# Layer 0's expert blocks in eight turns of nine, with scatters ahead of them, fetches and adding up behind them, and the capacity search at three bits a turn

## The reference, cut to what is computed

```python
xn = _layernorm(x, axis=-1)
x = x + _L0_attn_ref(xn, ...) + _L0_ffn_ref(xn, ...)   # 16 rows of 256 tokens; t = 4096
...
def _L0_ffn_ref(x, Wr, W1, W2):                        # EMBED 128, FFN 512, N_EXPERTS 8, TOP_K 2
    probs = jax.nn.softmax(xf @ Wr, axis=-1)
    topk_probs, topk_experts = jax.lax.top_k(probs, TOP_K)
    cap = max(math.ceil(t * TOP_K * CAP_FACTOR / N_EXPERTS), 1)      # 1280
    for e in range(N_EXPERTS):
        ...
        vals, idx = jax.lax.top_k(g_masked, cap)
        g = jnp.where(jnp.isfinite(vals), vals, 0.0)
        h = jax.nn.relu(xf[idx] @ W1[e]) @ W2[e]
        y = y.at[idx].add(g[:, None] * h)
```

## Time and profile before

| what | value |
|---|---|
| median of 3 runs | 2079.53 us (2074.1 to 2083.88) |
| the profiled execution | 2077.18 us, span 2074.8 us |
| PE busy | 1624.0 us, 78% of the span |
| DVE, ACT, POOL busy | 1238.6, 766.0, 380.3 us |
| mean granted TensorE clock | 0.86 |
| stretches | layer 0 to about 662 us, layer 1 to about 1070, layer 2 to about 1610, then layer 3 |

### The profile page before, as it was taken

The page is one execution under the profiler, slowest core; times in us unless marked ns, Lnnn a source line. Parts: engine busy times, 40 slices in busy tenths (PEclk is TensorE's granted clock), DMA queues, the critical chain, the costliest instruction groups (busy, mean ns, idle before and its releaser), DMA issues.

```text
span 2074.8 us, 44343 instructions
## 1 busy us (share of the span) xinstructions
PE 1624.0 (78%) x12567; PEld 1050.6 (51%) x12567; DVE 1238.6 (60%) x3512; ACT 766.0 (37%) x1723; POOL 380.3 (18%) x488
## 2 busy tenths in 40 slices
PE   3257999999972599998983588888887688888888
PEld 3123666666632577877872244444543344444444
DVE  6454666566675665665574455555557566666664
ACT  2013445445441222322230254445454144434444
POOL 1274101101167011111123300000006200000000
PEclk9855999999965698988885598999997599999999
DMA  7023455455421000000001332333232111111110
GB/s 233 28 70 101 141 155 174 137 157 174 130 58 37 0 1 1 0 0 0 0 1 40 89 95 89 98 112 110 82 95 57 36 39 42 40 40 39 37 40 15
DMA packets 133278, 144.90 MB, mean 70 GB/s; under 512 B 15001, under 2 KB 114130, under 8 KB 132946
## 3 DMA queue, kind: packets, MB, share of 16 engines
q1 hardware_dynamic: 127058, 131.37, 21.4%
q0 software_dynamic: 6144, 12.60, 2.1%
HBM read 104.65 MB, written 39.52 MB: 69 GB/s over the span
## 4 chain that ended last, share of the span: by engine, by line
PE 48%; DVE 19%; issue 13%; DMA 8%; POOL 7%; SPq 2%; ACT 2%; DVEq 1%; ACTq 0%; POOLq 0%
PE pO L694 6%; DMA stk<-packed_qk 6%; PE pT_ L557 5%; PE pH L584 5%; PE pY L592 5%; DVE X L1278 4%; PE pH L500 4%; POOL sorted_x L910 3%; PE pS L642 3%; PE pS L664 3%; DVE mx L1239 2%; PE pT_ L490 2%; PE pY L512 2%; PE pT_ L555 2%; DVE stk L1245 2%
## 5 line engine op out<-in xcount | busy, mean ns | idle before, releaser
L804 ACT ACTIVATE pex<-pT_ 128x512 f32<-128x512 f32 (+1 forms) x768 | 426.6, 562 | 656.1 <-PE pT_ L557 362.8
L1239 DVE TENSOR_REDUCE mx<-pS 128x2 f32<-128x512 f32 x512 | 348.2, 688 | 194.9 <-PE pS L540 176.8
L557 PE MATMUL pT_<-stk 32*128 32x256 f16 x1024 | 208.2, 298 | 120.0 <-DMA stk<-packed_qk 67.0
L540 PE MATMUL pS<-stk 32*128 32x256 f16 x1024 | 220.3, 304 | 23.4 <-DMA stk<-packed_qk 19.6
L694 PE MATMUL pO<-pex,va 128*9 128x256 f32 (+1 forms) x3072 | 218.4, 408 | 2.0 <-ACT pex L804 2.0
L797 ACT ACTIVATE wb<-pH,b 128x256 f32<-128x256 f32 x256 | 107.3, 470 | 268.4 <-PE pH L500 268.4
L883 POOL TENSOR_TENSOR qk<-qkf,qk 128x512 f16<-128x512 f32 x48 | 55.4, 1155 | 779.5 <-DVE qk L1211 407.3
L557 PEld LDWEIGHTS pT_<-stk 32*128 32x128 f16 x1024 | 55.9, 94 | 238.0 <-issue 87.3
L500 PE MATMUL pH<-XT,w 128*128 (+1 forms) x512 | 146.7, 413 | 0.0
L584 PE MATMUL pH<-xsT,wb 128*128 128x128 f32 x888 | 134.1, 297 | 0.0
L1245 DVE SCALAR_TENSOR_TENSOR stk<-pS,stk 128x512 f16<-128x512 f32 x96 | 66.3, 691 | 109.2 <-PE pS L664 105.0
(11 more groups left out here) (195 smaller groups left out, 2841.5 us busy)
## 6 DMA issues: line engine op xcount, KB each, us to landing
wb<-in_w SPq DMA_DIRECT2D x111, 514.0 KB, 3.8
stk<-packed_qk SPq DMA_DIRECT2D x96, 256.0 KB, 2.8
packed_qk<-qk SPq DMA_DIRECT2D x144, 128.0 KB, 2.0
xsb<-sorted_x SPq DMA_DIRECT2D x111, 64.0 KB, 3.4
sorted_y<-ysb SPq DMA_DIRECT2D x111, 64.0 KB, 3.1
sorted_x<-wb SPq DMA_DIRECT2D x2, 2048.0 KB, 13.3
w<-in_w SPq DMA_DIRECT2D x2, 1024.0 KB
out<-X SPq DMA_DIRECT2D x16, 128.0 KB, 1.8
```

The lines of the kernel that those rows point to most:

```text
L540: return pe.matmul(bank[:, part * T:(part + 1) * T], stk[rows, side, j, part * P:(part + 1) * P], stk[rows, side, j, T:2 * T], start=True, ...
L557: return pe.matmul(bank[:, part * T:(part + 1) * T], key, stk[rows, side, j, 0:T], start=True, stop=True)
L804: act.activation(pex[:, k % 8, 0:n], bank[:, 0:n], ACT.Exp).then_inc(s("T_free"), 1)
L1239: ins = dve.tensor_reduce(mx[:, :, j, col], bank.rearrange("p (c n) -> p c n", c=2), AX.X, ALU.max)
```

## The change

Layer 0's 72 blocks come in turns 3 to 10, nine each, and the ring of loads has 3 places. Scatters: 6 behind turn -2, 13 in turn -1 (at S), 15 each in turns 0, 1 and 2 (at D). Fetches: one a head in turns 11 to 15. DVE adds 28 of the 32 tiles in turns 12 to 15, one every second head, and 4 behind the turns. The search does three bits a turn in turns 1 to 10 (a C and four c steps each) and the choice among equal ones is in turn 11. Layer 0's loop runs over turns 3 to 10, the others' as before. The places are zeroed 24 blocks at a time, since wb is smaller. Layer 2 keeps its plan.

```diff
-IN_FLIGHT = {0: 4, 2: 3}
+IN_FLIGHT = {0: 3, 2: 3}
...
-BLOCKS_A_TURN = {0: 6, 2: 3}
-BLOCK_TURNS = {0: range(2, 14), 2: range(1, 14)}
-SORT_TURNS = {0: range(-2, 2), 2: range(-2, 0)}
-SEARCH_STEPS = 6
-CAPACITY_TURN = 14
-
-GATHERS_A_HEAD = {14: 3, 15: 4}
-TILES_A_HEAD = {0: 1, 2: 2}
+ZEROED_BLOCKS = 24
+BLOCKS_A_TURN = {0: 9, 2: 3}
+BLOCK_TURNS = {0: range(3, 11), 2: range(1, 14)}
+SCATTERS = {0: {-2: 6, -1: 13, 0: 15, 1: 15, 2: 15}, 2: {-2: 16, -1: 16}}
+SEARCH_STEPS, SEARCHES_A_TURN = 5, 3
+SEARCH_TURNS = range(1, 11)
+CAPACITY_TURN = 11
+
+GATHER_FROM = {0: (11, 0), 2: (14, 2)}
+GATHERS_A_HEAD = {0: {11: 1, 12: 1, 13: 1, 14: 1, 15: 1}, 2: {14: 3, 15: 4}}
+COMBINE_FROM = {0: 12, 2: 15}
...
-LOOP_FROM, LOOP_TO = 2, 14
+LOOPS = {0: (3, 11), 1: (2, 14), 2: (2, 14), 3: (2, 14)}
...
-            if layer == 0 and n in SEARCH_TURNS and h % 8 < SEARCH_STEPS:
+            if layer == 0 and n in SEARCH_TURNS and h < SEARCHES_A_TURN * SEARCH_STEPS:
...
-                k, part = divmod(h, 8)
+                k, part = divmod(h, SEARCH_STEPS)
...
-                    sorting = l in SORTED and turn.loop is None and turn.n in SORT_TURNS[l]
+                    sorts = SCATTERS[l].get(turn.n, 0) if l in SORTED and turn.loop is None else 0
+                    gathers_now = GATHERS_A_HEAD[l].get(turn.n, 0) if l in SORTED and turn.loop is None else 0
+                    if gathers_now:
+                        pool.wait_ge(s("S_free"), PRIMED + turn.use("S"))
+                        pool.wait_ge(s("row_staged"), PRIMED + min(B, turn.n + 2))
                     for kind, k, local in turn.steps:
-                        if sorting and turn.n > -2 and kind == "S":
+                        if kind == ("S" if turn.n < 0 else "D") and k < sorts and turn.n > -2:
                             scatter(1)
...
                         if kind == "D":
-                            if l in SORTED and turn.loop is None and turn.n in GATHERS_A_HEAD and (turn.n, k) >= (14, 2):
-                                gather(GATHERS_A_HEAD[turn.n])
+                            if gathers_now and (turn.n, k) >= GATHER_FROM[l]:
+                                gather(gathers_now)
...
-                    if sorting and turn.n == -2:
-                        scatter(NT // 2)
+                    if turn.n == -2:
+                        scatter(sorts)
...
-                for part in {1: (1, 2), 2: (3,), 3: (4,), 4: (5,), 5: (6,)}[k]:
+                for part in {1: (1, 2), 2: (3,), 3: (4,), 4: (5, 6)}[k]:
...
+            def combined_at(l, n, h):
+                turns = B - COMBINE_FROM[l]
+                first, last = ((NT * (H * (n - COMBINE_FROM[l]) + hh)) // (H * turns) for hh in (h, h + 1))
+                return [t for t in range(first, last) if t < 2 * (B - 2)]
...
-            for c in range(0, MAXBLOCKS, NT):
-                n = min(NT, MAXBLOCKS - c)
+            for c in range(0, MAXBLOCKS, ZEROED_BLOCKS):
+                n = min(ZEROED_BLOCKS, MAXBLOCKS - c)
```

More of the change, by code:

```diff
@@ L63 @@
 MAXBLOCKS = max(BLOCKS.values())
-BLOCKS_A_TURN = {0: 6, 2: 3}
-BLOCK_TURNS = {0: range(2, 14), 2: range(1, 14)}
-SORT_TURNS = {0: range(-2, 2), 2: range(-2, 0)}
-SEARCH_STEPS = 6
-CAPACITY_TURN = 14
-GATHERS_A_HEAD = {14: 3, 15: 4}
-TILES_A_HEAD = {0: 1, 2: 2}
+ZEROED_BLOCKS = 24
[8 more added lines that the diff above has]
+COMBINE_FROM = {0: 12, 2: 15}
 GATHERS = 8
 WROW = 2 * FF + NF
-SEARCH_TURNS = range(-1, 14)
 def blocks_of(layer, n):
@@ L207, in use, with run_turns @@
         return self.loop * (2 * ring_uses(self.layer, ring, self.n)) + before
-def run_turns(eng, layer, body, loop_to=LOOP_TO):
+def run_turns(eng, layer, body, unlooped=0):
     last = B if layer == 1 else B + 1
-    for n in range(-2, LOOP_FROM):
+    loop_from, loop_to = LOOPS[layer][0], LOOPS[layer][1] - unlooped
+    for n in range(-2, loop_from):
         body(Turn(layer, n))
-    with eng.Fori(0, (loop_to - LOOP_FROM) // 2) as loop:
+    with eng.Fori(0, (loop_to - loop_from) // 2) as loop:
         for par in range(2):
-            body(Turn(layer, LOOP_FROM + par, loop))
+            body(Turn(layer, loop_from + par, loop))
     for n in range(loop_to, last):
@@ L245, with __init__ @@
 class TurnChain(Chain):
-    def __init__(self, eng, sem):
+    def __init__(self, eng, sem, layer):
         super().__init__(eng, sem)
         self.total, self.counts = 0, {}
+        self.loop_from, self.loop_to = LOOPS[layer]
     def enter(self, turn):
@@ L256, in enter @@
         else:
-            per = self.counts[LOOP_FROM - 1]
+            per = self.counts[self.loop_from - 1]
             self.base = turn.loop * (2 * per) + self.total
@@ L264, in leave @@
         if self.turn.loop is not None:
-            assert self.n == self.counts[LOOP_FROM - 1], (self.n, self.counts)
-            if self.turn.n == LOOP_FROM + 1:
-                self.total += self.n * (LOOP_TO - LOOP_FROM) - self.n
+            assert self.n == self.counts[self.loop_from - 1], (self.n, self.counts)
+            if self.turn.n == self.loop_from + 1:
+                self.total += self.n * (self.loop_to - self.loop_from) - self.n
                 return
@@ L598, in take_turn @@
                     elif kind == "C":
-                        pe.wait_ge(sem("counted"), PRIMED + turn.count(2, k + 3))
+                        first = SEARCHES_A_TURN * SEARCH_TURNS[0] - 1
+                        pe.wait_ge(sem("counted"), PRIMED + turn.count(SEARCHES_A_TURN, k - first))
                         pe.matmul(bank[:, 0:8], onesm[:, :], cnt[:, :], start=True, stop=True)\
@@ L845, in _ @@
                     pool.wait_ge(sem("gates"), PRIMED + l + 1)
-                split = TurnChain(pool, sem(f"L{l}_pool_chain"))
+                split = TurnChain(pool, sem(f"L{l}_pool_chain"), l)
                 def stage(turn, par):
@@ L922, in gather @@
                             pool.wait_ge(sem(f"ys_out{ring}"), PRIMED + 16 * n_out)
-                        pool.wait_ge(s("S_free"), PRIMED + Turn(l, 14).use("S"))
-                        pool.wait_ge(s("row_staged"), PRIMED + B)
                     for t, choice in gathers[:n]:
@@ L936, in _ @@
                     if l == 0:
-                        pool.wait_ge(sem("places_zeroed"), 16 * -(-MAXBLOCKS // NT))
+                        pool.wait_ge(sem("places_zeroed"), 16 * -(-MAXBLOCKS // ZEROED_BLOCKS))
                     pool.wait_ge(sem("places_ready"), 1 + SORTED.index(l))
@@ L1229, in take_turn @@
                     elif kind == "D":
-                        if l in SORTED and turn.n == B - 1:
-                            n_add = TILES_A_HEAD[l]
-                            combine(l, final, stats, [t for t in range(n_add * k, n_add * (k + 1)) if t < 2 * (B - 2)])
+                        if l in SORTED and turn.n >= COMBINE_FROM[l]:
+                            combine(l, final, stats, combined_at(l, turn.n, k))
                     elif kind == "S":
@@ L1366, in _ @@
                 final, stats = {}, {}
-                tc = TurnChain(dve, sem(f"L{l}_dve_chain"))
+                tc = TurnChain(dve, sem(f"L{l}_dve_chain"), l)
                 run_turns(dve, l, lambda turn: take_turn(turn, tc))
@@ L1370, in _ @@
                 if l in SORTED:
-                    combine(l, final, stats, range(min(TILES_A_HEAD[l] * H, 2 * (B - 2)), NT + 2))
+                    combine(l, final, stats, range(2 * (B - 2), NT + 2))
         primed = [n for n in sems if n in SHARED_SIGNALS or (n.startswith("L") and not n.endswith("_chain"))]
@@ L1461, in _ @@
                     sp.wait_ge(sem("fixed_rows"), 16 * (1 + l // 3))
-                run_turns(sp, l, sp_turn, LOOP_TO - 2)
+                run_turns(sp, l, sp_turn, 2)
             sp.wait_ge(sem("stored"), 16 * B)
```

## The result

The changed kernel takes 2411.45 us (median of 4 runs, 2405.8 to 2414.66) against 2078.12 us of the kernel before: 1.160 times as long, 95% interval 1.1563 to 1.1635. The prediction said slower, 2369 us, range 2265 to 2455. The direction and the mechanism came out as forecast; one term of the sum, the clock, was too small by a third.

A forecast was written before the change was run, and what follows sets the result against it. PE bounds the turns with blocks (busy 29.0 of 30.7 us). Layer 0's turns sum to 821.6 against 486.9 us, +334.7; with -12.2 and -30.5 that is +292.0 on 2077.2: 2369 us, range 2265 to 2455.

The forecast's parts named there:

- the clock: Turns 3 to 10: four waits of 3.8 us or more lower PE's clock, 2.6 us each, 10.2 a turn.
- The ring of three: Turns with nine blocks: X waits for tokens whose load only an earlier Y lets go, 25.1 us a turn.
- Rival 2's first half: Turns with nine blocks: all seven waits of over 1 us lower the clock, 18.2 a turn, 2433 us; chance 0.15.
- Rival 1: Turns with nine blocks: waits cost only themselves, no clock is lost, 63.4 us a turn, 2287 us; chance 0.15.
- rival 2's second half: Turns with nine blocks: work between waits can't win the clock back, 90.5 us a turn, 2504 us; chance 0.10.
- Rival 3: Turns with nine blocks: the load is covered ahead of X6 and X7, 38.3 us a turn, 2087 us; chance 0.05.
- Rival 4: Layer 0's ends: blockless turns take longer (+25) or the tail stays (+30), 2390 to 2420 us; chance 0.10.
- The head: Turn 0 starts 12.2 us earlier, with 6 scatters on POOL after turn -2 instead of 16.
- The first turn with blocks: PE's 9.6 us wait for the last scatter and the low clock around it stay, 12 us added.
- Turns 1 and 2, 14 and 15: Layer 0's blockless turns: turns 1 and 2 take 29.6 us each, turns 14 and 15 take 40.4 together.
- The end: Behind layer 0's attention: all fetches are out by turn 14, next layer begins at 631.5 instead of 662.0, -30.5 us.

The follow-up runs named there:

- Experiments 1: Changed kernel with tokens of block k+3 issued behind X of block k, only the weights behind Y: 2114.02 us, 1.0189 of the kernel before.
- 2: Kernel before with a ring of three alone, places zeroed 24 blocks at a time: 2355.98 us, 1.1351 of the kernel before.
- 11: Kernel before with a ring of three and tokens of block k+3 let go by X of block k instead of Y: 2073.85 us, 0.9987.
- experiment 3: Changed kernel with the two DMAs of a load swapped, tokens ahead of weights: 2260.78 us, 1.0896 of the kernel before.
- experiment 12: Kernel before with 6 scatters instead of 16 behind turn -2, the ten left over in turn 1: 2076.71 us, 0.9987.

## Why the prediction was right, and where it was short

Profiled against profiled, the steps of the sum:

```
                                   predicted   measured
turn 0 starts earlier by                12.2       12.6
turn 0                                  26.4       26.3
turns 1 and 2                           59.2       63.9
eight turns with nine blocks           600.8      629.3
  of it first one longer by               12        5.3
  a turn: PE's work                     38.3       38.3 (taken from the forecast)
  a turn: waits for tokens              25.1       25.4
  a turn: the clock                     10.2       15.0
turn 11                                 35.6       36.3
turns 12 and 13                         59.2       60.0
turns 14 and 15                         40.4       46.8
first to last exponential              821.6      862.6
gain at the end                         30.5       29.9
```

*The ring of three* held as worked out. The prediction put waits at X3 to X8 and X1, none at X0 and little at X2; the trace has seven a turn, 25.4 us against 25.1. One by one, in turn 5, X3 to X8 wait 3.5, 3.3, 1.8, 4.7, 4.6 and 4.3 us and X1 2.3, where the forecast had 2.8, 3.8, 2.4, 4.7, 4.7, 4.4 and 1.7. Experiments 1, 2 and 11 show it from three sides: take the rule away and 297 us go, put the ring alone into the kernel before and 279 come, and put both in and nothing is lost.

*The clock* is the step that was mis-sized: 15.0 us a turn (78.7 - 38.3 - 25.4; 15.5 by PE's busy time, see experiment 1) where I had 10.2. The price of one wait was near, and the number of them wrong. I let only the four waits of 3.8 us or more lower the clock, at 2.6 each, since layer 2's 3.1 us were the shortest that I had seen do it. The windows of six us behind each wait show which of them pay: 55 of the 57 in the changed kernel (all but one of 1.3 and one of 1.8 us), all 44 in experiment 2, of which the shortest was 1.7 us, and 34 of the 49 in experiment 3. Spread over these, the cost is 2.2, 2.4 and 2.4 us each, near the 2.6 of the forecast. No wait of over 2.2 us went without a stretch at 0.50 behind it; of the shorter ones some did, and no run here shows what decides it. Rival 2's first half said nearly that, all seven waits at 2.6, for 2433 us; the measurement is 22 below it and 42 above my number. The Trainium skill (TensorE: Matmul & The Clock Gate, HAM oscillation — how this bites in real kernels) tells of a kernel whose waits for a DMA, about 3 to 5 us each, let every tile restart at the half rate; the long waits here agree with it, and the shorter ones, down to 1.4 us in the changed kernel, lie outside what it tells and mostly pay as well. Rival 1 (no clock cost, 2287) falls with the mean of 0.70. So does rival 2's second half (half clock throughout, 2504): by that mean 60% of the time was at half.

*Rival 3*, the load covered, was rightly held for unlikely, and experiment 1 is that case made: 2114 us where I had 2087. 18 of the difference lie in layer 0 (its block turns 1.4 us longer each, and 9 us in the turns without blocks), the rest behind it.

*Rival 4*, that the ends don't pay (2390 to 2420), has the measured 2411 in its band, but not for its reason: the turns without blocks took 12.5 us more than forecast, not 25, and the gain at the end came.

*The head.* Turn 0 starts 12.6 us earlier, so the step was right; experiment 12 shows that in the kernel before it would have been worth nothing, because the last scatter sets when blocks start. The sum could subtract the 12.2, since it adds the third turn ahead of the blocks (32.8 us) elsewhere, but a gain it is not in the change either: the last scatter is issued at 208.0 where it was at 189.2.

*The first turn with blocks* is 5.3 us longer than the mean of the other seven, not 12; 4.6 of that are waits for tokens (29.4 us against 24.8). In experiment 1, whose other turns hardly wait, it is 9.7 longer: where every turn waits and is at a low clock, a first wait adds less. I should not have added the whole 12 to a turn that had its waits counted already.

*Turns 1 and 2, 14 and 15* took 11.1 us more than forecast; the clock's miss is 8 x 4.8, 38 us. Turn 15 ran at clock 0.50 for 18.5 us, where turn 15 before took 15.2 at 0.72 and experiment 1's 14.8 at 0.73. In turns 1 and 2, DVE is busy for 19.4 and 19.9 us against 18.1 with three C a turn in place of two; whether that is the cause wasn't tried.

*The end* was right, 29.9 against 30.5: no fetch behind attention's end.

*What the change could have brought.* Turn 4's 30.7 us less six blocks of 2.44 is 16 us of PE work in a turn without blocks, but such a turn takes 26 to 36 at clock 0.50 to 0.66 in the changed kernel. The change makes four more of them. With the tokens let go in time that and the gains at the ends leave 1.9% over the kernel before on the first chip, 0.7% on another. No version here was faster than the kernel before beyond its interval.

## What to carry to other kernels

Before a ring is shortened or its schedule compressed, write down for each place which instruction lets it go and what work stands between that one and the first reader of the next content; it has to be longer than release, issue and landing together. Where one place holds several buffers, let each go by its own last reader, and issue the small load that is wanted first ahead of the large one. And add to each wait that PE meets in the midst of dense work the clock that it loses, here some 2.4 us on top of the wait's own length, for most of the waits under 3 us too.

## What was unexpected of the hardware

- 64 KB of tokens land 3.4 us after their issue (median) when they are issued 0.5 us behind the 514 KB of weights, and 1.8 us after it when issued ahead. The Trainium skill (DMA: Bandwidth & Descriptors, Queues, rings and completion order) says that each DMA engine takes the descriptors of a ring in order; the 1.6 us between the two orders agree with it.
- Waits of at most 2.8 us, six a turn, go with a mean clock of 0.79 (experiment 3), against 0.96 with hardly any (experiment 1); PE was busy for 76% of that stretch. Two waits of about the same length can differ: the clock stayed full behind one of 2.11 us and fell to half behind one of 2.04.
- The same kernel before took 2077 and 2078 us on some chips and 2192 and 2196 us on two others, and every kernel profiled on those two shows unnamed waits, of up to 65 us, on ACT and DVE in written-out turns with indirect DMAs. The kernel before itself was not profiled there. A comparison across chips would have been wrong by more than the effect of most experiments here.
